# Moving ScalarE copies, gate sums, softmax and the gate's matmul later in the lora stage of an adaLN + routed-lora feed-forward kernel

## What is computed

```python
y      = einsum('bct,bcd->bdt', x, weights[condition])
base   = einsum('bsi,oi->bso', y, W_org)                       # 1024 -> 1024
q      = einsum('bi,ki->bk', y.mean(axis=1), Wq)
coeffs = softmax(einsum('bk,ek->be', q, lora_keys) / sqrt(128))
h      = einsum('bsi,eir->bser', y, lora_down)                 # 8 experts x 64
delta  = einsum('be,bser,ero->bso', coeffs, h, lora_up)
out    = x + base + delta
```

## Time and profile before

| | |
|---|---|
| median of 3 runs | 794.61 us |
| the profiled execution, its own time | 793.19 us |
| its span, first to last instruction | 791.4 us |
| busy share: TensorE, weight load, VectorE, ScalarE, GpSimd | 91%, 75%, 62%, 30%, 21% |
| chain that ended last, by engine | TensorE 73%, VectorE 16%, issue 7% |
| mean granted TensorE clock | 0.981 of full |

### The profile page before, as it was taken

One profiled execution on the slowest core, in us unless ns is written; L12 is line 12 of the kernel. 1 busy time (PEld: TensorE's weight loads), 2 busy tenths in 40 slices (PEclk: granted clock), 3 DMA queues, 4 the chain that ended last, 5 costly groups with the idle time before them and its releaser, 6 DMA issues.

```text
span 791.4 us, 10492 instructions
## 1 busy us (share of the span) xinstructions
PE 719.7 (91%) x3385; PEld 594.1 (75%) x3385; DVE 491.8 (62%) x757; ACT 237.6 (30%) x456; POOL 165.2 (21%) x141
## 2 busy tenths in 40 slices
PE   5697999999999999999995749999999999999997
PEld 4585887878878788787884637777777777777775
DVE  3579448374483744826445787776767677777673
ACT  4345235242351433514333431111111111111110
POOL 2431103012030020300200003322323232223232
PEclk9899999999999999999998969999999999999999
DMA  9952353344434434333321536666666666666642
GB/s 265 320 152 90 126 152 121 111 136 135 141 122 120 137 133 136 124 122 120 119 81 55 211 119 213 205 220 200 213 211 215 200 209 192 207 204 206 203 131 98
DMA packets 83672, 128.10 MB, mean 162 GB/s; under 512 B 18458, under 2 KB 51234, under 8 KB 81570
## 3 DMA queue, kind: packets, MB, share of 16 engines
q1 hardware_dynamic: 75024, 125.26, 48.6%
q10 hardware_dynamic: 8594, 2.17, 1.4%
HBM read 77.07 MB, written 50.33 MB: 161 GB/s over the span
## 4 chain that ended last, share of the span: by engine, by line
PE 73%; DVE 16%; issue 7%; DMA 1%; ACT 1%; POOL 1%; ACTq 1%; DVEq 0%; POOLq 0%; SPq 0%
PE x_ps L1282 21%; PE h_ps L1198 21%; PE w_ps L1282 10%; PE w_ps L1221 7%; PE y_ps L1176 6%; PE x_ps L1221 5%; DVE ba_l L760 4%; DVE blk L763 2%; DVE gs L763 1%; DVE tb_l L760 1%; DVE ga_l L760 1%; PE y_ps L1271 1%; DVE ysum L773 1%; DVE org_f L760 1%; DVE yg L791 1%
## 5 line engine op out<-in xcount | busy, mean ns | idle before, releaser
L459 POOL TENSOR_TENSOR blk<-blk,blkx 128x512 f32<-128x512 f32 x64 | 95.9, 1498 | 309.1 <-DMA blkx<-in_x_dram 155.6
L1282 PE MATMUL x_ps<-tb_h,ba_h 128*128 128x512 f32 x256 | 102.5, 400 | 29.5 <-DVE blk L763 28.4
L763 DVE TENSOR_TENSOR blk<-w_ps,blk 128x512 f32<-128x512 f32 x96 | 65.9, 687 | 61.3 <-PE w_ps L1282 32.5
L1198 PE MATMUL h_ps<-yq_h,down_h 128*128 128x512 f32 x256 | 101.8, 398 | 0.9 <-ACT ones_r L499 0.9
L1282 PE MATMUL x_ps<-tb_h,ba_l 128*128 128x512 f32 x256 | 100.3, 392 | 0.0
L1282 PE MATMUL x_ps<-tb_l,ba_h 128*128 128x512 f32 x256 | 100.2, 391 | 0.0
L1198 PE MATMUL h_ps<-yq_h,down_l 128*128 128x512 f32 x256 | 99.7, 390 | 0.0
L1198 PE MATMUL h_ps<-yq_l,down_h 128*128 128x512 f32 x256 | 99.7, 389 | 0.0
L843 DVE TENSOR_TENSOR g<-h_ps,coef 128x512 f32<-128x512 f32 x32 | 22.1, 691 | 117.7 <-PE h_ps L1198 98.3
L433 POOL TENSOR_TENSOR yq_l<-y_full,yq_h 128x512 fp32r<-128x512 f32 x32 | 46.3, 1448 | 198.7 <-ACT yq_h L499 198.7
L499 ACT ACTIVATE y_full<-y_ps 128x512 f32<-128x512 f32 x58 | 34.6, 597 | 163.3 <-PE y_ps L1176 163.3
(11 more groups left out here) (91 smaller groups left out, 1238.9 us busy)
## 6 DMA issues: line engine op xcount, KB each, us to landing
x_sb<-in_x_dram SPq DMA_DIRECT2D x32, 512.0 KB, 4.0
y_dram<-y_full SPq DMA_DIRECT2D x64, 256.0 KB, 2.7
r_dram<-blk SPq DMA_DIRECT2D x64, 256.0 KB, 2.4
yb<-y_dram SPq DMA_DIRECT2D x32, 512.0 KB, 7.5
blk<-r_dram SPq DMA_DIRECT2D x16, 1024.0 KB, 6.8
blkx<-in_x_dram SPq DMA_DIRECT2D x32, 512.0 KB, 6.9
out_dram<-blk SPq DMA_DIRECT2D x64, 256.0 KB, 4.0
x_sb<-in_L_ffn_W_org_dram SPq DMA_DIRECT2D x8, 512.0 KB, 3.8
```

Source lines behind the costliest of these rows:

```text
L459: pool.tensor_tensor(blk[p % 3][:, b, :], blk[p % 3][:, b, :], blkx[:, h, n, :], ALU.add).then_inc(x_added, 1)
L763: nc.vector.tensor_tensor(dst, a, b, ALU.add).then_inc(done, 1)
L1198: mm = nc.tensor.matmul(h_ps[:, m % 2, :], down[w][:, k, m * P:(m + 1) * P], yq[s][:, k, :], start=(k == 0 and i == 0), stop=(k == KC - 1 ...
L1282: mm = nc.tensor.matmul(bank, ba[s][n][:, k, :], tb[w][n][:, k, :], start=(first and k == 0 and i == 0), stop=(k == 3 and i == 2), skip_gr ...
```

## The change

On all engines some steps of a group's lora stage stand later in their list, and two copies earlier:

- ScalarE: the high part of S4 for P3 of j0 goes behind `take_r(j0, 2)` (and so does, in group 0, the high part of lora_up's P4 operand); `take_r(j0, 1, P3)` goes ahead of the high part of S1 for P5 of j1; `split_z` goes from behind `split_y(n + 2)` to behind `split_y(n + 3)`; `exps` goes behind `split_y(n + 7)`.
- VectorE: `gate_sums` goes behind `end_c22(j0)` and two low parts; `end_c21(j0)` ahead of one low part; `split_z` behind `split_y(n + 2)`; `softmax_first` from ahead of `end_c11(j1)` to behind `lo_block(j1, P4)` and `split_y(n + 6)`, right ahead of `end_c22(j1)`.
- TensorE: `make_scores` behind P2 and P5 of j1.

No instruction is added or removed.

```diff
@@ ScalarE
-                hi_sum(j0, P3, 3)
                 if more:
                     split_y(n)
-                    if q == 0:
-                        split_up(P4, 4)
                 else:
                     act.wait_ge(org_a, 4)
                     split_org(P1)
                 hi_block(j1, P1, 0, 0)
                 take_r(j0, 2, P6, r2_ready)
+                hi_sum(j0, P3, 3)
+                if q == 0:
+                    split_up(P4, 4)
                 hi_block(j0, P4, 1, 1)
@@
                 if more:
                     split_y(n + 2)
-                    split_z(q + 1)
                 else:
                     take_org(5)
                 hi_block(j1, P2, 0, 1)
                 take_r(j1, 0, P1, r1_ready)
+                take_r(j0, 1, P3, c12_ready)
                 hi_sum(j1, P5, 0)
                 if more:
                     split_y(n + 3)
-                take_r(j0, 1, P3, c12_ready)
+                    split_z(q + 1)
                 hi_sum(j1, P7, 2)
@@
                 if more:
                     split_y(n + 6)
-                    exps(q + 1)
@@
                 take_r(j1, 3, P5, r4_ready)
                 if more:
                     split_y(n + 7)
+                    exps(q + 1)
@@ VectorE
                 lo_block(j0, P4, 1, 1)
-                if more:
-                    gate_sums(q + 1)
-                else:
+                if not more:
                     sum_org(4)
                 end_c22(j0)
                 lo_sum(j1, P6, 1)
                 lo_block(j1, P2, 0, 1)
                 if more:
-                    split_z(q + 1)
+                    gate_sums(q + 1)
                 else:
                     sum_org(5)
                 sum_4(j1)
+                end_c21(j0)
                 lo_sum(j1, P5, 0)
                 if more:
                     split_y(n + 2)
-                end_c21(j0)
+                    split_z(q + 1)
                 lo_sum(j1, P7, 2)
                 if not more:
                     sum_org(6)
                 lo_sum(j1, P3, 3)
                 if more:
                     split_y(n + 4)
-                    softmax_first(q + 1)
                 end_c11(j1)
                 lo_block(j1, P4, 1, 1)
                 if more:
                     split_y(n + 6)
+                    softmax_first(q + 1)
                 else:
                     sum_org(7)
                 end_c22(j1)
@@ TensorE
                 up_6(j1)
-                if more:
-                    make_scores(q + 1)
                 up_2(j1)
                 up_5(j1)
+                if more:
+                    make_scores(q + 1)
                 up_7(j1)
```

More of the change, by code:

```diff
@@ L1367, in _ @@
                 up_6(j1)
+                up_2(j1)
+                up_5(j1)
                 if more:
                     make_scores(q + 1)
-                up_2(j1)
-                up_5(j1)
                 up_7(j1)
```

## The result

The changed kernel has a median of 814.66 us over 4 runs (812.9 to 815.47) against 794.62 us, a ratio of 1.0247 (95% interval 1.0229 to 1.0265): 20.0 us slower, where +16.2 had been forecast. Its profiled execution took 813.96 us, with a span of 812.1 against 791.4 us: 20.7 more.

What follows compares the result with a forecast made beforehand. TensorE was taken as the bound, busy throughout h stages and 19.83 of 20.89 us in the lora stage; 7 x 2.0 + 2.2 = +16.2 us took 793.19 to 809.4, median 810.8 us, range 803 to 819.

Steps and rivals of the forecast that it cites:

- The S4 part, +0.50 us a group: First half of the lora stage: VectorE's low part of S4 starts 0.50 us later, and P3 of j0 with it.
- Gate sums out of the way of `end_c22(j0)`: Before P4 of j0: without the 1.76 us gate sums its wait goes; gain over both gaps about 0.24 us.
- `end_c22(j1)` 2.1 us late: Second half of the lora stage: P4 of j1 starts 2.1 us after TensorE is free, +2.0 us a group.
- The three stalls: VectorE blocked by GpSimd on the shared SBUF port before end_c22(j1): 0.49, 1.09, 1.0 us; 1.6 more than before.
- Group 7, +2.2: Last group: later VectorE work delays turn_org(5) by 1.85 and turn_org(7) by 0.34 us, sum +2.2 us.
- rival B: TensorE after the 2.1 us idle: clock falls to 1.2 GHz, 1.4 us a group, up to 10 more, 820; chance 0.1.
- The clock in group 0: Group 0: clock taken to stay up, as after 2.59 us idle in the earlier trace; group forecast +2.0 us.
- A, fewer stalls: GpSimd instructions fall beside PSUM reads or reductions: one stall fewer gives 804, no surplus 800; chance 0.15.
- C, faster: At sum_1(j1), VectorE's queued instruction keeps the port ahead of GpSimd: -8 us, 786; chance 0.04.

Runs made afterwards that it cites:

- s4_only: Kernel before with only the high part of S4 (in group 0 also lora_up's P4 operand) moved later on ScalarE: 800.7 us, ratio 1.0075.
- softmax_back: Changed kernel with softmax_first put back ahead of end_c11(j1) on VectorE: 814.75 us, ratio 1.0254 to the kernel before.
- gate_in_h_again: Second run of gate_in_h, the same kernel, beside another version on one chip: 788.36 us, ratio 0.9927.
- gate_in_h: Kernel before with gate sums, z splits, scores and softmax moved out of the lora stage into the next group's h stage: 786.85 us, ratio 0.9912.
- split_late: Also gate_in_h_split_late: gate_in_h with ScalarE's split_y(n + 1), which releases GpSimd's first subtraction, moved behind take_r(j0, 3): 790.45 us, ratio 0.9965.
- s4_back: Changed kernel with the high part of S4 (in group 0 also lora_up's P4 operand) back ahead of split_y(n) on ScalarE: 808.18 us, ratio 1.0182.
- c22_first: Changed kernel with end_c22(j1) ahead of softmax_first on VectorE: 806.66 us, ratio 1.0151 to the kernel before.

## Why the prediction was right, and where it was short

- **The S4 part, +0.50 us a group.** Right: VectorE's low part waited 0.42 us for ScalarE (333.92), P3's wait went from 0.62 to 1.13, and s4_only shows this step by itself.
- **Gate sums out of the way of `end_c22(j0)`.** Right in kind and size: no wait at P4 of j0, `end_c22(j0)` 0.37 us idle behind ScalarE's copy (forecast 0.39). P6 of j1 begins 12.16 us into the stage instead of 12.40, the 0.24 us that were forecast; the stalls behind it took them back.
- **`end_c22(j1)` 2.1 us late.** Right: 2.02. The three stalls ahead of it, forecast as 0.49, 1.09 and 1.0 us, came on the instructions named: 0.92 for 0.42, 1.85 for two, 1.30 for 0.42. Taking GpSimd's reads away removed the wait, and putting the softmax back did not. The Trainium skill's "SBUF — State Buffer", "Who interferes with whom", puts the condition at two SBUF inputs on VectorE against a GpSimd instruction that reads; the runs agree on both sides (the softmax's subtraction takes 0.23 us inside a fill, 1.12 against a GpSimd subtraction).
- **Group 7, +2.2.** Measured +2.39, of which the waits forecast (5.38 and 2.74 us) make 2.20.
- **The term that was mis-sized: the clock,** which the sum left out and rival B priced at "up to 7 x 1.4 = 10 more". It was neither none nor all. In the profiled execution it fell behind 2 of the 6 waits of groups 1 to 6, at 1.6 us each, which is 3.2 of the 4.5 us by which the span exceeds the forecast. In softmax_back's it fell behind 3 of 7, the h products there taking 6.6 to 6.7 instead of 5.4 us.
- **The clock in group 0.** P1 of j1 took 2.5 us behind 3.71 us idle, and P3 of j0 was slow too: +2.8 instead of +2.0. The forecast had read from one trace that the clock stays up behind 2.59 us there. That was luck of the execution: of six others with this wait (2.58 to 2.60 us), it fell in four, among them gate_in_h_again but not gate_in_h, which are the same kernel. The longer wait of 3.71 us doesn't decide it either: in softmax_back P1 and P3 behind it ran at the upper level. So a fall behind such a wait should have been in the sum as a cost times a chance.
- **The page on the clock.** The Trainium skill's "TensorE: Matmul & The Clock Gate", "HAM oscillation — how this bites in real kernels", warns of idle gaps between bursts; those of its example are longer, waits for DMA. The trace agrees that they can bring the lower clock, but 4 of the 6 gaps of 1.9 to 2.0 us here did not; so rival B's "every group could pay it" did not come.
- **The rest:** 0.05 us a group and 0.3 us ahead of group 0's lora stage more, 0.3 us in the second pass less. No run tells its cause; four executions of the changed kernel lie 2.6 us apart.
- **Rivals.** A, fewer stalls, did not come, though split_late and gate_in_h show how movable they are. C, faster, hung on VectorE keeping the port ahead of GpSimd; it did not, and `sum_1(j1)` took 1.51 us again.

## What to carry to other kernels

- When an instruction is moved off an engine's critical list, follow the same list to its next deadline. All that stood ahead of `end_c22(j1)` still did. Before the change it had 0.65 us of slack (0.18 us waiting for P7, and 0.47 us from its end to P4). With the wait at P4 of j0 gone TensorE comes 0.7 us sooner and VectorE, idle at `end_c22(j0)`, 0.4 us later, so this slack was gone before any further stall. The 0.5 us of the S4 part shift both engines alike, as s4_back shows.
- A copy advanced ahead of another is worth nothing if it was waiting for TensorE, and the one put behind it inherits the wait.
- Work for the next stage belongs where the engine has room: the same gate, moved a stage further into the 29 us in which VectorE is busy for 9.4, gave 0.9%, where moving it within the stage, together with the small moves beside it, cost 1.8% (s4_back). And two engines that block each other are best arranged by putting the short urgent instruction ahead of the other's release, rather than by delaying the release: the delay cost a full stall at all four places.

## What the runs showed of the hardware that was not expected

- The fall of TensorE's clock is not decided by the length of a gap alone. Behind the waits of 1.9 to 2.0 us before P4 of j1, all behind the same dense work, it fell in 2 of 7 groups of the changed kernel, 1 of 7 in s4_back and 3 of 7 in softmax_back. Behind those of 1.2 to 1.3 us (c22_first) it never fell in seven groups. The same kernel profiled twice shows it in group 0, in gate_in_h and then in gate_in_h_again:

```profile
69.79 0.50 PE L1219 MATMUL x_ps<-tu_h,ga_h 128*128 128x512 f32 x1 [2.58 <-ACT blk L499]
...
70.16 0.79 PE L1219 MATMUL x_ps<-tu_h,ga_h 128*128 128x512 f32 x1 [2.58 <-ACT blk L499]
70.75 0.63 PE L1219 MATMUL x_ps<-tu_h,ga_l 128*128 128x512 f32 x1
```

The gap is the same, 2.58 us; the granted clock behind it is 1.00 in the one (69.79 to 73.20) and 0.50 in the other (70.16 to 73.20).
- In both falls of the changed kernel in groups 1 to 6 the product after the gap still began at the upper level (0.50, 0.39 us), and the lower came later: by 1.0 us (at 192.29) and by 1.5 us (at 298.19, behind 296.65).
- A GpSimd fill with zeros over the same area did not hold up a VectorE subtraction with two SBUF operands that lay wholly inside it (0.23 us).
- The length of a stall depends on where the two meet: in gate_in_h three of the four GpSimd subtractions fell beside PSUM reads and idle time and cost VectorE 0.4 us or nothing; in gate_in_h_split_late the last three came 0.6 to 0.9 us earlier in the stage, and each cost 1.1.
